# Token order and value bias moved to TensorE in the linear q, k, v stage, and the weights of the chosen experts moved to GpSimd in the projection stage

## The reference, cut to what matters

```
logits = x @ router_weight.T                       # x: 8192 x 256, 64 experts
scores = sigmoid(logits)
top_idx = top_k(scores + expert_bias, 6)
top_scores = take_along_axis(scores, top_idx)
probs = top_scores / (sum(top_scores) + 1e-20)
```

```
q, k, v = split(x @ W_qkv + b_qkv)
q = elu(q * 16 ** -0.5) + 1.0001
k = elu(k) + 1.0001
```

## Time and profile before

| | us |
|---|---|
| median of 3 runs | 3260.66 |
| profiled execution, its own time | 3258.48 |
| its span | 3256.8 |
| busy PE / DVE / ACT / POOL in the span | 2842.0 / 2225.7 / 1603.0 / 731.5 |
| prj, 1141 to 1344 us of the span (203 us): busy PE / DVE / ACT / POOL | 158.9 / 164.1 / 92.5 / 63.2 |
| lqk, 1700 to 1940 us of the span (240 us): busy PE / DVE / ACT / POOL | 185.2 / 211.6 / 131.9 / 101.7 |

### The profile page before, as it was taken

How to read it: one execution, slowest core, us unless ns; L and a number is a source line. 1 busy time by engine, 2 the same in 40 slices (tenths; PEclk the granted TensorE clock), 3 DMA queues, 4 the chain that set the end, 5 groups by cost and what they waited for, 6 DMA issues and landing times. The chain is left out here.

```text
span 3256.8 us, 59136 instructions
## 1 busy us (share of the span) xinstructions
PE 2842.0 (87%) x20033; PEld 2062.9 (63%) x20033; DVE 2225.7 (68%) x6134; ACT 1603.0 (49%) x2446; POOL 731.5 (22%) x882
## 2 busy tenths in 40 slices
PE   7959999999999387689947777998399999999998
PEld 6834444444444276578836664555388888888887
DVE  6768999999997388663338883444466666666664
ACT  3506777777777244333325544544244444444443
POOL 1022222222222133247744422222000000000000
PEclk9959999999999666699968888999699999999999
DMA  6984556666662377648857867653432424243331
GB/s 244 330 153 83 108 115 112 112 112 116 112 110 65 127 270 269 214 138 225 221 165 269 296 228 228 183 162 100 132 99 74 122 65 117 78 102 92 90 86 46
DMA packets 342662, 485.87 MB, mean 149 GB/s; under 512 B 58832, under 2 KB 203248, under 8 KB 342384
## 3 DMA queue, kind: packets, MB, share of 16 engines
q1 hardware_dynamic: 331776, 468.94, 52.1%
q0 software_dynamic: 10240, 14.16, 2.3%
q10 hardware_dynamic: 496, 0.84, 0.1%
HBM read 278.77 MB, written 204.53 MB: 148 GB/s over the span
## 5 line engine op out<-in xcount | busy, mean ns | idle before, releaser
L551 ACT ACTIVATE att_pr<-att_e_ps 128x1024 f32<-128x1024 f32 (+2 forms) x640 | 567.3, 938 | 203.8 <-PE att_e_ps L603 203.8
L579 PE MATMUL att_m_ps<-att_ks,att_qs 63*128 63x512 f32 (+3 forms) x1536 | 465.9, 433 | 40.2 <-PEq L41 31.7
L513 DVE CUSTOM_DVE_ANT_0 att_kept<-att_m_ps,att_causal 128x256 f32<-128x256 f32 (+3 forms) x1024 | 448.5, 488 | 50.3 <-DVEq L41 21.9
L579 PEld LDWEIGHTS att_m_ps<-att_ks,att_qs 63*128 63x128 f32 x1536 | 234.3, 189 | 370.6 <-DVE att_mx L516 148.5
L492 POOL TENSOR_SCALAR_AFFINE_SELECT att_pr<-att_pr 128x256 f32<-128x256 f32 (+1 forms) x384 | 181.4, 485 | 698.0 <-PEq L594 694.5
L516 DVE TENSOR_REDUCE att_mx<-att_m_ps 128x1 f32<-128x512 f32 x512 | 323.3, 684 | 21.5 <-PE att_m_ps L579 17.5
L623 PE MATMUL att_o_ps<-att_pr,att_vs 128*32 128x512 f32 (+3 forms) x3072 | 328.7, 501 | 3.7 <-issue 2.0
L2604 ACT ACTIVATE fin_hh<-fin_hid 128x512 fp32r<-128x512 f32 x192 | 121.4, 632 | 399.8 <-DVE fin_hid L2450 302.2
L603 PE MATMUL att_e_ps<-att_qs,att_ks 64*128 64x512 f32 (+3 forms) x1536 | 269.1, 376 | 6.7 <-ACT att_pr L551 3.3
L2343 POOL TENSOR_TENSOR fin_rs<-fin_ve,fin_mhalf 128x4 f32<-128x4 f32 x48 | 48.4, 1007 | 928.6 <-POOLq L41 928.6
L2446 DVE TENSOR_TENSOR fin_hid<-fin_gate,fin_u_ps 128x512 f32<-128x512 f32 x192 | 131.5, 685 | 136.4 <-ACT fin_gate L2598 82.9
(11 more groups left out here) (332 smaller groups left out, 6921.2 us busy)
## 6 DMA issues: line engine op xcount, KB each, us to landing
fin_raw<-weights SPq DMA_DIRECT2D x32, 1024.0 KB, 9.6
att_qs<-q_high SPq DMA_DIRECT2D x128, 128.0 KB, 5.2
att_ks<-k_high SPq DMA_DIRECT2D x128, 128.0 KB, 6.5
attended<-att_ot SPq DMA_DIRECT2D x64, 256.0 KB, 8.5
acc<-att_zero SPq DMA_DIRECT2D x64, 256.0 KB, 2.2
moe_w<-w SPq DMA_DIRECT2D x128, 128.0 KB, 3.4
lqk_a<-acc SPq DMA_DIRECT2D x32, 512.0 KB, 6.0
attended<-lin_ot SPq DMA_DIRECT2D x32, 512.0 KB, 3.7
```

Of the source, the lines that this page charges most:

```text
L513: e.tensor_tensor_reduce(kept[:, n % MBUF, 0:w], m_ps[:, n % MBUF, 0:w], causal[:, BLK - w:], 1.0, -3e38, ALU.add, ALU.max, mx[:, h, at, q ...
L551: e.activation(out, src, ACT.Exp).then_inc(exp_done, 1)
L579: e.matmul(m_ps[:, (2 * i + n) % MBUF, 0:w], qs[rows, j, p, q * P:(q + 1) * P], ks[rows, j, p, h * BLK:h * BLK + w], start=True, stop=True ...
```

## The change

In prj DVE keeps the choice and leaves the weights to POOL, as a new last step of POOL's iteration: masked scores, then a sum over 64 by six halvings, then a power of -1 in place of the reciprocal, then the product. `mask_ready` and `mask_read` pass the mask to and fro. DVE also stops copying the best six (`pick`): the maximum is taken over a row that has two padding values of 3e38 behind the 64 scores.

In lqk PE's moving operand is read through `in_order`, so `qk` comes out in the order (q, tile) and DVE reads without a step. The bias of v is added by PE: a matmul of ones [2, 128] with the bias's high and low part [2, 512] opens the accumulation of two tiles. The 24 products that follow add to it. ACT copies `vp` to `vo`. PE waits for SP's word that `vo` was written (`v_read`). At the phase's start DVE splits the bias, and one small DMA moves its low part to the second partition.

```diff
@@ prj, gpsimd, at the end of stages
+                    if d is not None:
+                        j = d[1]
+                        e.wait_ge(mask_ready, 1)
+                        step(e.tensor_tensor(sc[:, j], sc[:, j], mask[:], ALU.mult))
+                        e.sem_inc(mask_read, 1)
+                        src, n = sc[:, j], E // 2
+                        while n:
+                            step(e.tensor_tensor(half[:, :, 0:n], src[:, :, 0:n], src[:, :, n:2 * n], ALU.add))
+                            src, n = half, n // 2
+                        step(e.tensor_scalar(ssum[:], half[:, :, 0], 1e-20, None, ALU.add))
+                        step(e.tensor_tensor(ssum[:], ssum[:], minus1[:], ALU.pow))
+                        e.tensor_tensor(xn[:, j, :, C:XW], sc[:, j], ssum[:].unsqueeze(2).broadcast_to((P, TPB, E)),
+                                        ALU.mult).then_inc(weights_ready, 1)
@@ prj, vector
-                    step(e.tensor_copy(pick[:, :, 0:K], top[:, :, 0:K]))
...
+                    e.wait_ge(mask_read, 1)
+                    e.tensor_scalar(mask[:], rep[:, :, 0:E], -1e38, None, ALU.is_lt).then_inc(choice_ready, 1)
+                    step.settle()
+                    e.sem_inc(mask_ready, 1)
...
-                    if d is not None:
-                        weigh(d[1])
@@ lqk, vector
-                                e.scalar_tensor_tensor(phi[:, j, k].rearrange("p (q t) -> p q t", t=TPB),
-                                                       in_order(qk[:, k]), bqk1[:, k:k + 1], in_order(ex[:, k]),
-                                                       ALU.add, ALU.max).then_inc(phi_done, 1)
-                        e.wait_ge(v_ready, 1)
-                        for f in range(2):
...
+                                e.scalar_tensor_tensor(phi[:, j, k], qk[:, k], bqk1[:, k:k + 1], ex[:, k], ALU.add,
+                                                       ALU.max).then_inc(phi_done, 1)
@@ lqk, scalar, ahead of kt
+                        e.wait_ge(v_ready, 1)
+                        for f in range(2):
+                            cols = slice(f * P, (f + 1) * P)
+                            i = e.activation(vo[:, c[1], f].rearrange("p t (h d) -> p t h d", d=VW)[:, :, :, 0:HD],
+                                             vp[:, :, cols].rearrange("p t (h d) -> p t h d", d=HD), ACT.Copy)
+                        i.then_inc(vo_ready, 1)
@@ lqk, tensor
-                                    (lambda k: xh[:, j, k], lambda k: xl[:, j, k]), KC).then_inc(qk_ready, 1)
+                                    (lambda k: in_order(xh[:, j, k]), lambda k: in_order(xl[:, j, k])), KC
+                                    ).then_inc(qk_ready, 1)
...
+                        e.wait_ge(v_read, 1)
                         for t in range(TPB):
+                            if t % 2 == 0:
+                                e.matmul(vp[:, t:t + 2], one[:], bvs[:], start=True, stop=False)
```

More of the change, by code:

```diff
@@ L847, in phase_project_route @@
         weights_ready = ph.sem("weights_ready")
+        mask_ready = ph.sem("mask_ready")
+        mask_read = ph.sem("mask_read")
         xo_seen = ph.sem("xo_seen")
@@ L938, in _ @@
                 step(e.memset(mhalf[:], -0.5))
+                step(e.memset(minus1[:], -1.0))
                 e.sem_inc(pe_consts, 1)
@@ L955, in stages @@
                         take(e, (yvar_ready, 1), (x_loaded[j], 16), (xo_stored[j], 16), (yn_ready, 1))
+                    if d is not None:
[11 more added lines that the diff above has]
+                                        ALU.mult).then_inc(weights_ready, 1)
+                        take(e, (mask_ready, 1))
+                        step.close()
+                e.sem_inc(mask_read, 1)
                 pipeline(e, stages, 4)
@@ L1006, in choose @@
                     for t in range(TPB):
-                        e.max(top[:, t], sb[:, t, 0:E])
+                        e.max(top[:, t], sb[:, t])
                     step.settle()
-                    step(e.tensor_copy(pick[:, :, 0:K], top[:, :, 0:K]))
                     for t in range(TPB):
-                        e.match_replace(rep[:, t], pick[:, t], sb[:, t], -3e38)
+                        e.match_replace(rep[:, t], top[:, t], sb[:, t], -3e38)
                     step.settle()
[L1014 to L1019, removed]
-                    take(e, (scores, 1))
[L1022 to L1029, removed]
+                    e.wait_ge(mask_read, 1)
+                    e.tensor_scalar(mask[:], rep[:, :, 0:E], -1e38, None, ALU.is_lt).then_inc(choice_ready, 1)
+                    step.settle()
+                    e.sem_inc(mask_ready, 1)
+                    take(e, (mask_read, 1))
+                    take(e, (scores, 1))
                 def stages(a, b, c, d):
@@ L1556, in phase_linear_qkv @@
         bqk1 = ph.sb("bqk1", [P, 4])
-        bv = ph.sb("bv", [P, C])
+        bv = ph.sb("bv", [2, 2, C])
+        bvs = ph.sb("bvs", [2, 2, C], f32r)
+        bvl = ph.sb("bvl", [1, 2, C], f32r)
+        onef = ph.sb("onef", [2, P])
+        one = ph.sb("one", [2, P], f32r)
         ident = ph.sb("ident", [P, P])
@@ L1609, in phase_linear_qkv @@
         vo_ready = ph.sem("vo_ready")
+        v_read = ph.sem("v_read")
         x2_stored = [ph.sem(f"x2_stored{j}") for j in range(2)]
@@ L1701, in _ @@
                 split_weights(e, step, wf, wh, wl)
+                step(e.tensor_copy(bvs[:], bv[:]))
+                step(e.tensor_tensor(bvl[:], bv[0:1], bvs[0:1].bitcast(fp32), ALU.subtract))
+                e.sem_inc(bias_low, 1)
+                step(e.memset(onef[:], 1.0))
+                step(e.tensor_copy(one[:], onef[:]))
                 e.sem_inc(pe_consts, 1)
-                e.wait_ge(ones_ready, 1)
                 step.close()
@@ L1802, in _ @@
                 e.wait_ge(pe_consts, 2)
+                e.wait_ge(bias_moved, 16)
+                e.sem_inc(v_read, 1)
                 def stages(a, b, c):
```

26 lines of the change are left out of this document (14 added, 12 removed).

## The result

The changed kernel takes 3280.2 us (median of 7 runs, 3274.7 to 3290.3), the kernel before 3260.5 us (7 runs, 3248.7 to 3267.3): a ratio of 1.007, 95% interval 1.0055 to 1.0084, some 20 us slower. The forecast was 3284 us. The total came out, but its two terms didn't. Each phase is timed from its first instruction to that of the next, in one profile of each kernel.

The account below looks back on a forecast made before the run. DVE was taken to bound lqk, with POOL idle in prj. The forecast added +12 us in prj and +12 us in lqk, 24 us on 3260.7, giving 3284 us, with a range of 3243 to 3340.

Parts of the forecast that it names:

- The weights on POOL: In prj, POOL's ten new instructions in series, gaps included, take 5.36 us an iteration.
- The new loop is ... 14.4 us: In prj, POOL's queue becomes the bound: 14.4 us an iteration against 13.77, +0.63 us in some 13 iterations.
- the sentence on SP: In prj, the row's store and the next loads of x leave 3 to 4 us later, at no cost.
- POOL's queue and the last block: In prj, 8 us for the longer loop and 3.6 us before the last store, together +12 us.
- The step on PE: In lqk, 24 q and k matmuls reading with a 512-byte step take 0.45 us each instead of 0.23: +12 us.
- rival A: PE reads with a step for nothing: lqk 14.5 to 15.0 us an iteration, -15 to -22 us, kernel 3239 to 3266; chance 0.26.
- The main case: prj +3 to +25 us, lqk +6 to +28 at 17.0 us an iteration, kernel 3269 to 3311, middle 3284; chance 0.5.
- the exponentials, behind PE, would be late: In lqk, the path over PE and ACT's last exponential, not DVE, sets the iteration: 17.0 us against 16.1.
- The rule on lines: SBUF's 16-byte lines make PE pay for the step too; at twice the time 0.47 us a matmul, lqk some 19 us slower.
- `phi` at 0.69 us: In lqk, DVE's four phi fall from 1.127 to 0.69 us each without the step, 1.74 us together.
- rival D: The order isn't what makes phi slow; it stays near 1.1 us, changing nothing in the likeliest forecast; chance 0.05.
- `vo` on ACT for nothing: In lqk, ACT's two copies of some 0.65 us each fill its idle 4.32 us before kt, without a wait.

Follow-up runs that it names:

- e9: Changed kernel with prj's rows, choice and weights stored apart, each with its own semaphore, the rows' store ahead of the loads: 3249.6 us, ratio 0.9973 to before.
- e1: Kernel before with the whole lqk phase of the changed kernel, prj untouched: 3247.1 us, ratio 0.9960 to before.
- e2: Kernel before with the whole prj phase of the changed kernel, lqk untouched: 3296.6 us, ratio 1.0105 to before.
- e10: Kernel before with only the value bias moved to PE and the copy of v to ACT, token order left with DVE: 3252.6 us, ratio 0.9986.
- e12: Kernel before with the token order on PE, bias left with DVE, and SP's stores of phi and kt one step later: 3250.7 us, ratio 0.9971.
- e8: Changed kernel with prj's rows, choice and weights stored apart, each with its own semaphore, the rows' store behind the loads: 3256.9 us, ratio 0.9993 to before.

## Why the prediction was right in its sum and wrong in its terms

**The weights on POOL (forecast 5.36 us): right**, 5.11. The price by two rows with the same operation held for every step: 0.74 for 0.76, the halvings 1.98 for 1.91, the power 1.04 for 1.02, the product a little cheaper, 0.61.

**"The new loop is ... 14.4 us": a loop that exists, but not the one that ends last.** e9 shows it at 13.88. The failed step is the sentence on SP: "SP issues the row's store 3 to 4 us later, and with it the next loads of x, which are needed only a whole iteration on." I followed the loads behind the store, and not the store itself, whose landing frees the tile that `xn` writes. It had 1.1 us to spare before the change. The measured price is 29 us of the phase's 34. Of the 12 us that I forecast for POOL's queue and the last block, e9 leaves 5.

**The step on PE (forecast 0.45 us a matmul): mis-sized.** It is 0.273 to 0.283, where the turning point was stated as 0.41. So it was rival A's case, with a step that isn't quite free. A's iteration of 14.5 to 15.0 us, from the loads and ACT's chain, nearly holds 15.09, and its -15 to -22 us holds the -19.0. The loads act otherwise than in that sum, through the meeting of POOL's and DVE's additions; the prediction had it as up to 1 us on POOL's sum, and nothing on DVE. The main case's sum for one iteration put 24 x 0.17 us, 4 us, too much on PE. With it goes the claim that the exponentials, behind PE, would be late.

**The rule on lines.** The estimate from the rule of the Trainium skill ("SBUF — State Buffer", section "Specifications (TRN2)": two hits on a line of 16 bytes for full bandwidth) at twice the time, 0.47 us, was wrong for this operand; its sign was right, since the step costs 0.04 to 0.05 us. DVE's `phi` loses a third of its time when the step goes, PE's matmul takes a fifth more when it comes.

**`phi` at 0.69 us:** 0.746 by the profile, so nearly right; rival D is out. **`vo` on ACT for nothing:** it takes 1.09 us for the pair, and behind it ACT waits 0.92 us for the turned k; no cost was seen.

**The sum.** +12 and +12 were forecast; +34 and -19 came, and +12 in lin. One error was 22 us too low and the other 31 us too high, and a phase that wasn't touched made up the difference: 3284 was near by luck.

**What stays open.** lin isn't touched by any of the kernels. It took 308.8 us in before's profile and 309.5 to 325.4 in the other thirteen, and its length goes with its granted clock (correlation -0.93 over the fourteen). The windows of lin in before, and in after:

```profile
1962.32:2271.11 308.79, 279.55 (x3808) 169.59 (x3808) 127.06 (x258) 148.56 (x256) 82.37 (x133) 0.92 0.54 167
```
```profile
1975.40:2296.10 320.70, 288.87 (x3808) 173.68 (x3808) 127.05 (x258) 148.77 (x256) 82.28 (x134) 0.89 0.51 161
```

Kernels with a shorter lqk tend to have a longer lin, but weakly (correlation -0.51), and e1 gained 12 us by its median where its lqk gained 20; but e2, with lqk as before, had 316.7 too. Before's 308.8 is the lowest of all and stands on one profile, so the +12 in lin can't be put down to the change. Whether the faster phase gives its gain back through the clock of the next was not settled.

## What to carry to other kernels

When an instruction moves to an idle engine, follow its result to the last reader, the DMA included: what frees the buffer is the store's landing, not the engine. Give a late part of a tile its own tile and store, and put an urgent store ahead of the loads on its queue. Where DVE and GpSimd both work on SBUF, look at when they meet before adding up their times. Where a term rests on a price that no row shows, the turning point is worth more than the value taken, and a sum that comes out says nothing on its terms until each half has run alone.

## What the runs showed of the hardware

- A moving operand with a step of 512 bytes costs TensorE 0.046 us per 512 columns at 2.4 GHz (0.233 in e10, 0.279 in after), and nothing at 1.2 GHz (0.427 for both). The order on DVE, with the same step on its PSUM and its SBUF input, costs it 0.38 us (0.746 to 1.127).
- Two of DVE's operations, whose inputs all lie in SBUF, wait for a GpSimd addition that is already running: the clamp above, and the addition behind `xl`, 2.81 us on average in after and 1.31 in e12, where most of them meet none (groups by line below, after and e12). `phi` and `xl`, which have an input in PSUM, keep their length beside a GpSimd addition: 0.746 us for the 29 `phi` of e12 that meet one and 0.747 for the 35 others. In after POOL's second addition takes 3.2 instead of 2.4 us. The Trainium skill ("SBUF — State Buffer", "SBUF: two separate sides") says that the port pair of the two is an exclusive lock held for a whole instruction; these rows agree with it.

```profile
L1731 DVE TENSOR_TENSOR lqk_x<-lqk_x,lqk_yn 128x1024 f32<-128x1024 f32 x14 | 39.4, 2812 | 0.0
```
```profile
L1714 DVE TENSOR_TENSOR lqk_x<-lqk_x,lqk_yn 128x1024 f32<-128x1024 f32 x13 | 17.1, 1314 | 0.0
```

- Where a store stands in its queue sets when it lands: 640 KB took 3.5 us from the issue as the last of a block's transfers (after), 512 KB took 5.8 us with others close around it (e9), and 7.9 us right behind four loads of 256 KB (e8).
